# Both layer normalisations scaled on GpSimd, one-input conversions in its splits, and a new table of places

## The chip, the cores and the metric

The kernel runs on one core of a Trainium2 chip. The time is device microseconds of one launch. The time before is a median of 3 runs; the profile is of one further execution.

## The reference, cut to what matters

The input x is 8 batches of 1024 tokens of 256 columns, all in 32 bits. Every batch goes through three layers, each with a residual:

```python
x = x + 0.5 * ffn(layernorm(x), Wq, Wk, Wv, Wo, Wff)      # softmax attention, 16 heads of 16 columns
x = x + attn(layernorm(x), w_qkv, b_qkv, w_o, b_o)        # 8 heads of 32, no softmax
x = x + 0.5 * ffn(layernorm(x), Wq, Wk, Wv, Wo, Wff)

def layernorm(x):  return (x - mean(x)) / sqrt(var(x) + 1e-5)
def ffn(x):        # softmax(q k / 16) v per head, @ Wo, l2 normalise, @ Wff, l2 normalise, exact gelu
def attn(x):       # (q k^T) v per head, @ w_o + b_o
```

The middle layer has no softmax, so the kernel computes it from the Gram matrix of the normalised rows.

## The kernel before

There are 16 phases p. Phases 0 to 7 do the first softmax layer of batches 0 to 7, phases 8 to 15 the last one. A phase has 128 tiles, one for each head and each block of 128 keys, against all 1024 queries. For one tile TensorE makes the scores in a slot of PSUM (`ring`, three slots, line L798 of the profile), VectorE copies them to `exp_ring` and takes their minimum (L636), ScalarE takes the exponential in place and sums it (L563). For each four tiles (a group) VectorE takes the reciprocal of the sums (L646), GpSimd scales the values with it into `v_scaled` (L517, the step `recip` in its order), and TensorE multiplies (`av`, L809) into `o_acc`. `exp_ring` holds four groups, so the scores of a group wait for the product of the group four before.

Beside the tiles of phase p the engines work on its neighbours. For phase p - 1 they do what stands behind the attention: `u` (eight times, TensorE L746 into a slot, ScalarE squares L566 and L569, VectorE copy L653), `u_norm` and `w_norm` (reciprocal roots on GpSimd L524 to L535), `gelu` (ScalarE L574) and `x1` (VectorE L658). For phase p + 1 they do what stands ahead of it: `ln_stats`, `ln_aggr` and `ln_rstd` (VectorE, then one power on GpSimd, L491), `xn` (eight VectorE instructions that normalise `x_prep`, L686), `xt` (transposes L831, ScalarE copy L582), `qk` and `v`. Each `qk` piece of 128x512 is copied to `kq_stage` by ScalarE (L596) and then split on GpSimd into three bf16 parts by four instructions (L397, L399, L401, L403); SyncE's queue copies the parts to `kq_stack` by 32 DMAs for each quarter of a phase (L411). GpSimd does 125 of the 128 splits; ScalarE and VectorE do the other three, at the start.

In phases 1 to 8, called linear here after the name of their table, the middle layer of batch p - 1 is done as well: `ln2_stats`, `ln2_aggr`, `ln2_rstd`, `xn2` (eight VectorE instructions into `w_xn`, L700), `gram` (TensorE, L848, which waits for all eight), `xt2`, `T`, `VK`, `G`, `H`, `xbias` (GpSimd L539) and `y`. Phase 0 and phases 9 to 15 are called plain. The normalisation `xn` is done for phase 0 ahead of the first tile and then in phases 0 to 14.

Nothing is scheduled at run time. Each step has a place in a table (its unit is one tile of the phase), each engine's program is its steps sorted by place less a lead of the engine, and each engine runs its program in order:

```python
            place -= LEAD[engine].get(kind, 0)
            if engine == "pe":
                for part in range(parts):
                    placed.append((place + gap * part, n, part, step))
            else:
                placed.append((place + gap * (parts - 1), n, 0, step))
        return [(step, part) for _, _, part, step in sorted(placed)]
```

Of the kernel before, what the change touches and what calls it, by code (L numbers as in the profile page):

```python
# [5 lines left out]
def build_macaron(nc, x_in, w_qkv, b_qkv, w_o, b_o, Wq, Wk, Wv, Wo, Wff, out):  # L6
# [36 lines left out]
    def tokens(rows):  # L43
# [8 lines left out]
            "ln_stats": (11.5, 15, 15.4, 16.2, 16.3, 16.4, 17.2, 18.9),  # L52
            "ln_aggr": (22.2,),
            "ln_rstd": (28.2,),
            "xn": (31.6, 31.7, 37.7, 39.5, 42.3, 42.4, 55.3, 60.9),
            "xt": (44.7, 49.6),
            "qk": (64.4, 70.9, 72.5, 78.8),
            "v": (86.2, 95.3, 98.3),
            "setup": (66.7,),
            "weights": (103.6, 103.8, 108.6, 111.3),  # L60
            "stack0": (78.4,),
            "load_xp": (8.9,),
        },
        "PLAIN": {
            "recip": 5.7,
            "av": 9,
            "av_next": 2.5,
            "z": 6,
            "u": (8.5, 13, 16.4, 25.1, 32.5, 46.1, 55.5, 60.8),
            "u_norm": (61.9,),  # L70
            "w_norm": (67.5,),
            "gelu": (70.2,),
            "x1": (71.8, 72, 72.1, 72.2),
            "ln_stats": (7.1, 8.4, 9.2, 10, 11.9, 13.3, 13.5, 13.8),
            "ln_aggr": (21,),
            "ln_rstd": (24.2,),
            "xn": (32.3, 34.8, 36.2, 44.9, 45.7, 46.7, 57.1, 60.8),
            "xt": (62.1, 62.3),
            "qk": (78.9, 84.8, 93.3, 102.4, 21, 28.8, 37.5, 41.1),
            "v": (113.9, 119.5, 126.3, 5.4),  # L80
            "load_xp": (1,),
            "stack1": (3.2,),
            "load_xr": (5.4,),
            "stack2": (50.8,),
            "stack3": (60.1,),
            "stack0": (105.3,),
            "store": (109.5,),
# [5 lines left out]
            "z": 6.3,  # L93
            "u": (8.9, 9.9, 15.9, 16.3, 17.4, 22.3, 25.5, 27.6),
            "u_norm": (27.7,),
            "w_norm": (31.3,),
# [18 lines left out]
            "xt": (45.2, 46.3),
            "qk": (77.1, 81.7, 92.8, 97.6, 32.4, 35.9, 38.5, 42.5),
            "v": (111.5, 123.9, 127.1, 7.9),
            "load_xp": (1.9,),
            "stack1": (25.5,),
            "load_xr": (42,),  # L120
            "stack2": (59.3,),
            "stack3": (70.1,),
            "stack0": (100.7,),
            "store": (114.1,),
        },
        "TAIL": {
            "u": (8.4, 10.7, 20, 27.6, 33.6, 51.2, 59.7, 60.2),
            "u_norm": (23.8, 64.1),
            "w_norm": (35.6, 68.8),
            "gelu": (66.9, 90.5),  # L130
            "x1": (79.8, 81.3, 90.5, 96),
            "load_xr": (0.4,),
            "store": (136, 137.5),
        },
# [2 lines left out]
    LEAD = {"sp": {},
            "pe": {},
            "act": {"qk": 1.0, "u": 1.0, "xt2": 1.5, "gram": 1.5, "weights": 3.0, "G": 1.0, "xt": 0.5, "H": 1.5},
            "dve": {"ln_stats": -1.0, "VK": -0.5, "H": 0.5, "z": -0.5},  # L140
            "pool": {"recip": 0.5, "xn": 0.5, "x1": -1.5, "xbias": 2.5, "w_norm": 1.5, "qk": -0.5, "u_norm": -1}}
# [776 lines left out]
```

## Time and profile before

| | |
|---|---|
| median of 3 runs | 2936.62 us (2935.42 to 2938.29) |
| the profiled execution, its own time | 2938.12 us |
| span of its profile | 2936.3 us |
| VectorE busy | 2775.7 us, 95% |
| ScalarE busy | 2704.8 us, 92% |
| TensorE busy (matmuls) | 2692.5 us, 92% |
| GpSimd busy | 857.8 us, 29% |

An engine's busy time is the union of its instructions' records. On VectorE and ScalarE a record reaches some 0.08 us into the next one, so that of instructions without a gap the starts are nearer together than the records are long.

### The profile page before, as it was taken

The page shows a single profiled execution, that of the slowest core. Times are in us where ns is not written, and L with a number is a line of the kernel's source. Part 1 is how long each engine was busy: PE and PEld are TensorE (multiplying, and loading weights), DVE is VectorE, ACT ScalarE, POOL GpSimd, SP SyncE. Part 2 cuts the span into 40 slices and gives each one's busy share as a digit, 9 for nine tenths or more (in the row PEclk, how much of TensorE's full clock was granted, in tenths as well). Part 3 has the DMA queues.
Part 4 walks back from the last instruction along what each step waited for, and adds up shares of the span by engine and source line. Part 5 has one row for each costly group of instructions (what it writes and reads, how often), then busy time and mean ns, then how long its engine had stood idle before and what let it go on. Part 6 is the DMA issues. An engine that isn't in the chain of part 4 may idle for free.

```text
span 2936.3 us, 87317 instructions
## 1 busy us (share of the span) xinstructions
PE 2692.5 (92%) x35680; PEld 1062.6 (36%) x35680; DVE 2775.7 (95%) x5622; ACT 2704.8 (92%) x4983; POOL 857.8 (29%) x1181
## 2 busy tenths in 40 slices
PE   5899999999999999999999998998989899898987
PEld 2233443434434344343343433332333333333422
DVE  5999999999999999999999999999999999999987
ACT  4999998999989989999899999999999999999997
POOL 2323303332133232331323323232331323233121
PEclk8999999999999999999999999999999999999999
DMA  5231242313423234123331243422324342232440
GB/s 122 50 64 41 54 102 48 72 43 59 103 38 58 67 59 101 30 54 81 59 81 39 53 92 59 90 56 57 75 47 102 59 90 56 58 73 47 87 87 16
DMA packets 151362, 192.89 MB, mean 66 GB/s; under 512 B 34001, under 2 KB 85713, under 8 KB 150962
## 3 DMA queue, kind: packets, MB, share of 16 engines
q1 hardware_dynamic: 150386, 186.13, 31.1%
q8 instruction: 281, 4.60, 0.7%
q0 software_dynamic: 576, 1.18, 0.3%
q14 instruction: 119, 0.97, 0.1%
HBM read 36.18 MB, written 16.78 MB: 18 GB/s over the span
## 4 chain that ended last, share of the span: by engine, by line
DVE 41%; PE 26%; ACT 18%; issue 8%; SPq 5%; POOL 1%; DMA 1%; DVEq 0%; POOLq 0%; ACTq 0%
DVE exp_ring L636 33%; ACT exp_ring L563 14%; PE ring L746 10%; PE o_acc L809 7%; PE ring L798 7%; SPq L411 5%; PE ring L848 2%; ACT w_xn L574 2%; DVE bn_stats L676 1%; DVE w_xn L653 1%; DVE x_post L658 1%; DVE v_now L713 1%; DVE w_xn L700 1%; DVE exp_rsums L646 1%; PE ring L831 1%
## 5 line engine op out<-in xcount | busy, mean ns | idle before, releaser
L636 DVE TENSOR_SCALAR_CACHE_REDUCE exp_ring<-ring 128x1024 f32<-128x1024 f32 x2048 | 2411.1, 1213 | 82.9 <-PE ring L798 76.0
L563 ACT ACTIVATE exp_ring<-exp_ring,neg_max 128x1024 f32<-128x1024 f32 x2048 | 2337.4, 1144 | 149.5 <-DVE exp_ring L636 147.5
L798 PE MATMUL ring<-kq_stack 128*32 128x512 bf16 x16384 | 1190.7, 384 | 158.0 <-DVE exp_ring L636 122.6
L809 PE MATMUL o_acc<-exp_ring,v_scaled 128*32 128x512 f32 x8192 | 1079.6, 600 | 27.6 <-POOL v_scaled L517 21.8
L798 PEld LDWEIGHTS ring<-kq_stack 128*32 128x32 bf16 x16384 | 406.1, 96 | 1109.2 <-DVE exp_ring L636 524.8
L517 POOL TENSOR_TENSOR v_scaled<-v_now,exp_rsums 128x64 f32<-128x64 f32 x512 | 151.9, 297 | 1851.8 <-DVE exp_rsums L646 1843.4
L563 ACT ACTIVATION_READ_ACCUMULATOR exp_ring<-exp_ring,neg_max 128x1 f32 x2048 | 386.4, 189 | 0.0
L809 PEld LDWEIGHTS o_acc<-exp_ring,v_scaled 128*32 128x32 f32 x8192 | 251.1, 111 | 249.8 <-POOL v_scaled L517 46.3
L746 PE MATMUL ring<-ffn_wo_wowff,o_T 128*32 128x256 f32 x4096 | 243.9, 380 | 16.6 <-issue 9.1
L746 PE MATMUL ring<-xn_T,ffn_wqkv 128*32 128x512 f32 x2048 | 248.0, 604 | 9.0 <-DVE exp_ring L636 7.7
L746 PEld LDWEIGHTS ring<-ffn_wo_wowff,o_T 128*32 128x32 f32 x4096 | 129.3, 110 | 137.9 <-DVE exp_ring L636 46.0
L636 DVE DVE_READ_ACCUMULATOR exp_ring<-ring 128x1 f32 x2048 | 166.1, 81 | 0.0
L397 POOL TENSOR_TENSOR kq_parts<-kq_stage,zero 128x512 bf16<-128x512 f32 x125 | 129.9, 1039 | 90.3 <-ACT kq_stage L596 76.5
L399 POOL TENSOR_TENSOR kq_rest<-kq_stage,kq_parts 128x512 f32<-128x512 f32 x125 | 148.5, 1188 | 9.8
L403 POOL TENSOR_TENSOR kq_parts<-kq_rest,kq_parts 128x512 bf16<-128x512 f32 x125 | 146.1, 1168 | 9.8
L401 POOL TENSOR_TENSOR kq_parts<-kq_rest,zero 128x512 bf16<-128x512 f32 x125 | 131.1, 1049 | 9.8
L746 PE MATMUL ring<-ffn_wqkv,xn_T 128*32 128x256 f32 x2048 | 122.6, 381 | 7.6 <-DVE exp_ring L636 7.5
L746 PEld LDWEIGHTS ring<-xn_T,ffn_wqkv 128*32 128x32 f32 x2048 | 61.5, 113 | 162.2 <-issue 98.9
L646 DVE RECIPROCAL exp_rsums<-exp_sums 128x4 f32<-128x4 f32 x512 | 87.0, 170 | 2.0 <-ACT exp_ring L563 1.3
L746 PEld LDWEIGHTS ring<-ffn_wqkv,xn_T 128*32 128x32 f32 x2048 | 60.7, 109 | 70.9 <-DVE exp_ring L636 35.0
L596 ACT ACTIVATE kq_stage<-ring 128x512 f32<-128x512 f32 x125 | 72.5, 580 | 8.9 <-PE ring L746 8.9
L653 DVE COPY w_xn<-ring 128x256 f32<-128x256 f32 x128 | 53.2, 415 | 22.4 <-PE ring L746 22.2
(94 smaller groups left out, 1252.6 us busy)
## 6 DMA issues: line engine op xcount, KB each, us to landing
kq_stack<-kq_parts SPq DMA_DIRECT2D x2030, 64.0 KB, 2.4
x_post<-in_L_attn_x SPq DMA_DIRECT2D x8, 1024.0 KB, 6.0
x_slots<-x_post SPq DMA_DIRECT2D x8, 1024.0 KB, 5.4
x_prep<-x_slots SPq DMA_DIRECT2D x8, 1024.0 KB, 9.8
x_post<-x_slots SPq DMA_DIRECT2D x8, 1024.0 KB, 5.9
x_prep<-in_L_attn_x SPq DMA_DIRECT2D x7, 1024.0 KB, 7.8
out<-x_post SPq DMA_DIRECT2D x7, 1024.0 KB, 5.7
kq_stack<-kq_parts POOLq DMA_DIRECT2D x18, 64.0 KB, 4.6
```

Source lines behind the costliest of these rows:

```text
L397: ops.tensor_tensor(hi, piece, zeros, ALU.add).then_inc(done, 1)
L399: ops.tensor_tensor(rest, piece, hi, ALU.subtract).then_inc(done, 1)
L401: ops.tensor_tensor(mid, rest, zeros, ALU.add).then_inc(done, 1)
L403: ops.tensor_tensor(lo, rest, mid, ALU.subtract).then_inc(done, 1)
L411: queue.dma_start(stack[q % 2][FD * t:FD * (t + 1), :, c, :], parts[rows:rows + FD, kp:qp + 4:3 + qp - kp, :]).then_inc(done[q % 2], 16)
L517: nc.gpsimd.tensor_tensor(vsc[a][:, i % EG, :, a * FD:(a + 1) * FD], heads, rsum[:, i % EG, :].unsqueeze(2).to_broadcast([P, HQ, FD]), ALU ...
L563: nc.scalar.activation(e, e, ACT.Exp, bias=negmax[:, i % NM:i % NM + 1], scale=-1.0, accum_out=sums[:, g % EG, c:c + 1]).then_inc(exp_done, 1)
L636: nc.vector.tensor_scalar(E[:, (g % EG) * HQ + c, :].rearrange("p (b n) -> p b n", b=NB), ps, -1.0, None, ALU.mult, ALU.min, accum_out=neg ...
L646: nc.vector.reciprocal(rsum[:, i % EG, :], sums[:, i % EG, :]).then_inc(rsum_ready, 1)
L746: last = mm(out[k:k + COLS], lhsT[:, k:k + COLS], rhs, start=start, stop=stop)
L798: last = mm(ps[k:k + COLS, n, :], kq[:, 0, c, j * P + k:j * P + k + COLS], kq[:, 1, c, n * BANK:(n + 1) * BANK], start=True, stop=True)
L809: last = mm(O[32 * c:32 * c + 32, n, :], vsc[a][:, g % EG, c, :], E[:, (g % EG) * HQ + c, n * BANK:(n + 1) * BANK], start=(a == 0 and j == ...
```

## The change

Five things are changed. `xn` and `xn2` move from VectorE to GpSimd, with the same instruction. The two conversions of a GpSimd split, until now the sum of the piece and a broadcast zero, become one-input instructions (times 1.0, plus 0.0). `XT2` gets a buffer of its own, where it lay in `x_prep`; so the load of `x_prep` no longer waits for the last `y`, and the copy `xt2` waits for the `y` of the phase before it. Half of `kq_rest` goes away; the three first splits use `H` for it. And nearly all places, with some leads, have other numbers.

```diff
         def split(engine, ops, piece, rest, m, n, done, at):
-            zeros = zero[:, 0:1].to_broadcast([P, BANK])
             hi, mid, lo = pieces(m, n)
-            ops.tensor_tensor(hi, piece, zeros, ALU.add).then_inc(done, 1)
+            ops.tensor_scalar(hi, piece, 1.0, 0.0, ALU.mult, ALU.add).then_inc(done, 1)
...
-            ops.tensor_tensor(mid, rest, zeros, ALU.add).then_inc(done, 1)
+            ops.tensor_scalar(mid, rest, 1.0, 0.0, ALU.mult, ALU.add).then_inc(done, 1)
...
-                    if is_linear(p - 3):
-                        sp.wait_ge(filled["y"], nth("pe", "y", p - 3, 3))
...
+                elif kind == "xn":
+                    pool.wait_ge(rstd_ready, p + 1)
+                    nc.gpsimd.tensor_scalar(xp[:, i, :], xp[:, i, :], mv[:, i, 0:1], rstd[:, i:i + 1],
+                                            ALU.subtract, ALU.mult).then_inc(xn_ready, 1)
...
+                elif kind == "xn2":
+                    pool.wait_ge(rstd2_ready, p + 1)
+                    nc.gpsimd.tensor_scalar(wb[:, i, 0:D], xr[:, i, :], mv2[:, i, 0:1], rstd2[:, i:i + 1],
+                                            ALU.subtract, ALU.mult).then_inc(xn2_ready, 1)
...
-                elif kind == "xn":
-                    dve.wait_ge(rstd_ready, p + 1)
-                    nc.vector.tensor_scalar(xp[:, i, :], xp[:, i, :], mv[:, i, 0:1], rstd[:, i:i + 1],
-                                            ALU.subtract, ALU.mult).then_inc(xn_ready, 1)
...
-        XT2 = xp[:].rearrange("p (c t) d -> p c (t d)", c=DC)
+        XT2 = sb("xn2_T", [P, DC, N])
...
                 elif kind == "xt2":
-                    act.wait_ge(filled["xt"], nth("pe", "xt", p + 2, DC - 1))
+                    if p >= 1:
+                        act.wait_ge(filled["y"], nth("pe", "y", p - 1, 3))
...
-            "xn2": (45.5, 46.1, 46.9, 47.1, 47.2, 47.5, 49.4, 49.6),
+            "xn2": (44.1, 44.6, 45.5, 45.7, 45.8, 46.1, 47.8, 48.2),
...
-            "xn": (31.2, 32.7, 33.6, 34, 34, 34, 34.2, 34.4),
+            "xn": (31.1, 31.7, 32.6, 33.9, 33.9, 33.9, 34.1, 36.1),
```

On GpSimd, in the part of the third linear phase in which both norms of the phase before and the first splits are due, the program of before reads as follows (`rstd` is the power of `ln_rstd`, `sumsq_w` and `gelu_scale` are `w_norm`, the four `kq_` rows are one split):

```order
L517 TENSOR_TENSOR v_scaled<-v_now,exp_rsums 128x4x16
L491 TENSOR_TENSOR rstd<-rstd,minus_half 128x8
L533 TENSOR_TENSOR sumsq_w<-sumsq_w,minus_half 128x8
L535 TENSOR_TENSOR gelu_scale<-sumsq_w,u_rnorm 128x8
L397 TENSOR_TENSOR kq_parts<-kq_stage,zero 128x512
L399 TENSOR_TENSOR kq_rest<-kq_stage,kq_parts 128x512
L401 TENSOR_TENSOR kq_parts<-kq_rest,zero 128x512
L403 TENSOR_TENSOR kq_parts<-kq_rest,kq_parts 128x512
L517 TENSOR_TENSOR v_scaled<-v_now,exp_rsums 128x4x16
```

The same part of GpSimd's program after the change reads:

```order
L523 TENSOR_TENSOR v_scaled<-v_now,exp_rsums 128x4x16
L489 TENSOR_TENSOR rstd<-rstd,minus_half 128x8
L492 TENSOR_SCALAR x_prep<-x_prep,bn_mv,rstd 128x256
L539 TENSOR_TENSOR sumsq_w<-sumsq_w,minus_half 128x8
L541 TENSOR_TENSOR gelu_scale<-sumsq_w,u_rnorm 128x8
L492 TENSOR_SCALAR x_prep<-x_prep,bn_mv,rstd 128x256 x2
L397 TENSOR_SCALAR kq_parts<-kq_stage 128x512
L399 TENSOR_TENSOR kq_rest<-kq_stage,kq_parts 128x512
L401 TENSOR_SCALAR kq_parts<-kq_rest 128x512
L403 TENSOR_TENSOR kq_parts<-kq_rest,kq_parts 128x512
L523 TENSOR_TENSOR v_scaled<-v_now,exp_rsums 128x4x16
L492 TENSOR_SCALAR x_prep<-x_prep,bn_mv,rstd 128x256 x5
```

Three of the eight `xn` now stand between two scalings of the values, ahead of the first split, and five behind the second scaling.

Further on in the same phase, from the power of the second normalisation on, GpSimd's program before has one split and then only scalings:

```order
L494 TENSOR_TENSOR rstd<-rstd,minus_half 128x8
L397 TENSOR_TENSOR kq_parts<-kq_stage,zero 128x512
L399 TENSOR_TENSOR kq_rest<-kq_stage,kq_parts 128x512
L401 TENSOR_TENSOR kq_parts<-kq_rest,zero 128x512
L403 TENSOR_TENSOR kq_parts<-kq_rest,kq_parts 128x512
L517 TENSOR_TENSOR v_scaled<-v_now,exp_rsums 128x4x16 x9
```

After the change the eight `xn2` stand among these scalings:

```order
L496 TENSOR_TENSOR rstd<-rstd,minus_half 128x8
L397 TENSOR_SCALAR kq_parts<-kq_stage 128x512
L399 TENSOR_TENSOR kq_rest<-kq_stage,kq_parts 128x512
L401 TENSOR_SCALAR kq_parts<-kq_rest 128x512
L403 TENSOR_TENSOR kq_parts<-kq_rest,kq_parts 128x512
L523 TENSOR_TENSOR v_scaled<-v_now,exp_rsums 128x4x16
L499 TENSOR_SCALAR w_xn<-x_post,bn_mv,rstd 128x256 x7
L523 TENSOR_TENSOR v_scaled<-v_now,exp_rsums 128x4x16
L499 TENSOR_SCALAR w_xn<-x_post,bn_mv,rstd 128x256
L523 TENSOR_TENSOR v_scaled<-v_now,exp_rsums 128x4x16 x7
```

Seven of them run in one piece, with one scaling behind them and the eighth behind that.

VectorE's program at that place, between two reciprocals, read so before:

```order
L646 RECIPROCAL exp_rsums<-exp_sums 128x4
L700 TENSOR_SCALAR w_xn<-x_post,bn_mv,rstd 128x256
L636 TENSOR_SCALAR exp_ring,neg_max<-ring 128x1024
L700 TENSOR_SCALAR w_xn<-x_post,bn_mv,rstd 128x256 x2
L636 TENSOR_SCALAR exp_ring,neg_max<-ring 128x1024
L700 TENSOR_SCALAR w_xn<-x_post,bn_mv,rstd 128x256 x3
L636 TENSOR_SCALAR exp_ring,neg_max<-ring 128x1024 x2
L700 TENSOR_SCALAR w_xn<-x_post,bn_mv,rstd 128x256
L646 RECIPROCAL exp_rsums<-exp_sums 128x4
```

After the change only the tiles are left between such reciprocals, over more than five groups of four; two of the groups are:

```order
L653 RECIPROCAL exp_rsums<-exp_sums 128x4
L643 TENSOR_SCALAR exp_ring,neg_max<-ring 128x1024 x4
L653 RECIPROCAL exp_rsums<-exp_sums 128x4
L643 TENSOR_SCALAR exp_ring,neg_max<-ring 128x1024 x4
L653 RECIPROCAL exp_rsums<-exp_sums 128x4
```

In SyncE's queue the plain phases now issue `load_xr` ahead of the quarter `stack1`, and the store of the output ahead of `stack0` of the next phase; the linear phases keep their order there.

## Rows read from the trace of the kernel before

**Rows 1.** The page: busy time, share of the span and instructions.

```profile
PE 2692.5 (92%) x35680; PEld 1062.6 (36%) x35680; DVE 2775.7 (95%) x5622; ACT 2704.8 (92%) x4983; POOL 857.8 (29%) x1181
```

**Rows 2.** Windows: halves of a linear and a plain phase; columns as headed.

```profile
core 0: us, PE busy (x) PEld busy (x) DVE busy (x) ACT busy (x) POOL busy (x), PEclk, DMA share, GB/s
782.87:885.80 102.93, 95.63 (x1211) 39.58 (x1207) 98.09 (x214) 92.36 (x180) 30.03 (x39) 0.97 0.28 55
885.80:970.49 84.69, 83.49 (x1190) 35.07 (x1186) 81.97 (x156) 79.28 (x137) 27.21 (x36) 1.00 0.35 75
2064.58:2151.41 86.83, 81.44 (x1112) 31.31 (x1104) 84.86 (x181) 83.39 (x165) 27.74 (x38) 1.00 0.32 63
2151.41:2236.02 84.61, 75.21 (x960) 25.64 (x960) 81.12 (x156) 82.49 (x144) 22.30 (x32) 0.96 0.36 75
```

**Rows 3.** Waits, 782.87 to 885.80: us in total, times, longest.

```profile
ACT exp_ring L563 <- DVE exp_ring L636: 6.4, 10, 1.8
PE ring L798 <- DVE exp_ring L636: 3.4, 6, 1.1
DVE exp_ring L636 <- PE ring L798: 2.3, 4, 1.2
PE o_acc L809 <- POOL v_scaled L517: 2.2, 2, 1.9
```

**Rows 4.** Groups by line, same stretch: busy us, mean ns, idle before.

```profile
L686 DVE TENSOR_SCALAR x_prep<-x_prep,bn_mv,rstd 128x256 f32<-128x256 f32 x8 | 4.7, 631 | 0.0
L700 DVE TENSOR_SCALAR w_xn<-x_post,bn_mv,rstd 128x256 f32<-128x256 f32 x8 | 3.6, 475 | 0.0
L658 DVE SCALAR_TENSOR_TENSOR x_post<-w_xn,x_post 128x512 f32<-128x512 f32 x4 | 3.1, 781 | 0.0
```

**Rows 5.** Timeline of VectorE, then GpSimd, 824 to 830: start, us, what.

```profile
826.50 3.38 DVE L686 TENSOR_SCALAR x_prep<-x_prep,bn_mv,rstd 128x256 f32<-128x256 f32 x5
829.80 0.68 DVE L658 SCALAR_TENSOR_TENSOR x_post<-w_xn,x_post 128x512 f32<-128x512 f32 x1
...
825.36 1.17 POOL L399 TENSOR_TENSOR kq_rest<-kq_stage,kq_parts 128x512 f32<-128x512 f32 x1
826.61 1.19 POOL L401 TENSOR_TENSOR kq_parts<-kq_rest,zero 128x512 bf16<-128x512 f32 x1
827.88 1.15 POOL L403 TENSOR_TENSOR kq_parts<-kq_rest,kq_parts 128x512 bf16<-128x512 f32 x1
829.11 0.29 POOL L517 TENSOR_TENSOR v_scaled<-v_now,exp_rsums 128x64 f32<-128x64 f32 x1
```

**Rows 6.** Groups by line of a plain half, 2064.58 to 2151.41.

```profile
L686 DVE TENSOR_SCALAR x_prep<-x_prep,bn_mv,rstd 128x256 f32<-128x256 f32 x8 | 3.3, 412 | 0.0
```

**Rows 7.** Groups by line, whole span, GpSimd alone.

```profile
L517 POOL TENSOR_TENSOR v_scaled<-v_now,exp_rsums 128x64 f32<-128x64 f32 x512 | 151.9, 297 | 1851.8 <-DVE exp_rsums L646 1843.4
L397 POOL TENSOR_TENSOR kq_parts<-kq_stage,zero 128x512 bf16<-128x512 f32 x125 | 129.9, 1039 | 90.3 <-ACT kq_stage L596 76.5 <-DMA kq_stack<-kq_parts 13.4
L539 POOL TENSOR_TENSOR x_post<-x_post,bias_wide 128x512 f32<-128x512 f32 x32 | 40.9, 1288 | 16.7 <-DVE bias_wide L733 16.7
L491 POOL TENSOR_TENSOR rstd<-rstd,minus_half 128x8 f32<-128x8 f32 x16 | 26.3, 1643 | 6.9 <-DVE rstd L683 6.4
L485 POOL MEMSET v_scaled<- 128x512 f32 x2 | 1.0, 520 | 0.0
L480 POOL MEMSET identity<- 128x128 f32 x1 | 0.2, 201 | 0.0
```

**Rows 8.** Timeline of the start, VectorE and TensorE.

```profile
10.56 2.67 DVE L686 TENSOR_SCALAR x_prep<-x_prep,bn_mv,rstd 128x256 f32<-128x256 f32 x8 [1.85 <-POOL rstd L491]
11.12 4.07 PE L831 MATMUL ring<-identity,x_prep 128*128 128x128 f32 x16 [11.12 <-DVE x_prep L686]
```

**Rows 9.** Timeline of GpSimd, 819 to 857, first and last of interest.

```profile
819.88 1.64 POOL L491 TENSOR_TENSOR rstd<-rstd,minus_half 128x8 f32<-128x8 f32 x1
...
856.44 0.37 POOL L517 TENSOR_TENSOR v_scaled<-v_now,exp_rsums 128x64 f32<-128x64 f32 x1 [5.06 <-DVE exp_rsums L646]
```

More of the change, by code:

```diff
@@ L51, in build_macaron @@
         "START": {
[L52 to L62, printed above, removed]
+            "ln_stats": (12.7, 16.2, 16.6, 17.5, 17.6, 18.1, 18.4, 20.1),
@@ L63, in build_macaron @@
+            "ln_aggr": (26.8,),
+            "ln_rstd": (33.2,),
+            "xn": (35.1, 35.2, 40.4, 43, 45.8, 46.1, 58.8, 64.4),
+            "xt": (39.6, 45.6),
+            "qk": (64.5, 72.5, 74.5, 82.8),
+            "v": (88.2, 93.7, 97.6),
+            "setup": (60.2,),
+            "weights": (106.3, 107.2, 108.7, 113.8),
+            "stack0": (83.8,),
+            "load_xp": (11.3,),
         },
         "PLAIN": {
-            "recip": 5.7,
+            "recip": 5.4,
             "av": 9,
@@ L67, in build_macaron @@
             "av_next": 2.5,
-            "z": 6,
+            "z": 5.8,
             "u": (8.5, 13, 16.4, 25.1, 32.5, 46.1, 55.5, 60.8),
[L70 to L87, printed above, removed]
+            "u_norm": (61.8,),
+            "w_norm": (69.7,),
+            "gelu": (70.4,),
+            "x1": (71.8, 71.8, 72, 72.1),
+            "ln_stats": (6.5, 7.8, 8.9, 9.7, 11.6, 16.5, 16.7, 19.3),
@@ new lines, in build_macaron @@
+            "ln_aggr": (21.4,),
+            "ln_rstd": (26,),
+            "xn": (33.8, 34, 35.4, 44.1, 44.9, 48.5, 56.3, 60),
+            "xt": (61.1, 62.1),
+            "qk": (78.9, 84.8, 93.3, 102.4, 21.2, 28.9, 37.7, 41.3),
+            "v": (114.1, 119.7, 126.5, 5.9),
+            "load_xp": (0.1,),
+            "stack1": (4.3,),
+            "load_xr": (3.5,),
+            "stack2": (50.5,),
+            "stack3": (71.6,),
+            "stack0": (124,),
+            "store": (119.7,),
@@ L92, in build_macaron @@
             "av_next": 2,
[L93 to L96, printed above, removed]
+            "z": 5.1,
+            "u": (8.9, 9.9, 15.3, 16.3, 17.4, 22.3, 25.5, 27.6),
+            "u_norm": (27.9,),
+            "w_norm": (31.7,),
             "gelu": (32.6,),
-            "x1": (34.7, 35.4, 35.8, 36.6),
-            "ln2_stats": (36.4, 36.6, 37.3, 37.9, 38.1, 38.3, 38.4, 39),
+            "x1": (34.7, 35.5, 36, 36.6),
@@ L112, in build_macaron @@
-            "ln_aggr": (27.5,),
-            "ln_rstd": (29.6,),
-            "xn": (31.2, 32.7, 33.6, 34, 34, 34, 34.2, 34.4),
[L115 to L124, printed above, removed]
+            "ln2_rstd": (41.2,),
@@ new lines, in build_macaron @@
+            "xn2": (44.1, 44.6, 45.5, 45.7, 45.8, 46.1, 47.8, 48.2),
+            "gram": (52.4, 58.3),
+            "xt2": (65.9, 101.1),
+            "T": (63.1,),
+            "VK": (70.3,),
+            "G": (72.4,),
+            "H": (87.7,),
+            "xbias": (89.2, 90.3, 113.2, 115.7),
+            "y": (103.2, 107, 115.5, 119),
+            "ln_stats": (9.3, 14.5, 15.7, 16.1, 17.7, 20.7, 23.2, 26.4),
+            "ln_aggr": (27.4,),
+            "ln_rstd": (29.8,),
+            "xn": (31.1, 31.7, 32.6, 33.9, 33.9, 33.9, 34.1, 36.1),
@@ L125, in build_macaron @@
+            "xt": (44.3, 45.4),
+            "qk": (77.5, 81.7, 92.8, 97.6, 31.9, 35.9, 38.5, 41.1),
+            "v": (111.4, 123.8, 127, 7.9),
+            "load_xp": (10.8,),
+            "stack1": (25.4,),
+            "load_xr": (48.5,),
+            "stack2": (56.3,),
+            "stack3": (66.8,),
+            "stack0": (96.1,),
+            "store": (109,),
         },
         "TAIL": {
-            "u": (8.4, 10.7, 20, 27.6, 33.6, 51.2, 59.7, 60.2),
-            "u_norm": (23.8, 64.1),
@@ L129, in build_macaron @@
[L129 to L133, printed above, removed]
+            "u": (7.6, 8, 17.9, 25.7, 34.8, 52.6, 62, 62.2),
+            "u_norm": (19.1, 64.2),
+            "w_norm": (36.7, 68.8),
+            "gelu": (69.4, 89.1),
+            "x1": (72, 73, 82.2, 86.1),
+            "load_xr": (1.6,),
+            "store": (133.6, 137.6),
         },
     }
-    GAP = {'gram': 0.5, 'G': 0.5}
+    GAP = {'gram': 0.5, 'G': 1.0}
@@ L137, in build_macaron @@
     LEAD = {"sp": {},
             "pe": {},
[L139 to L141 removed]
+            "act": {"qk": 1.0, "u": 1.0, "xt2": 1.5, "gram": 2.5, "weights": 3.5, "G": 1.0, "xt": 1.0, "H": 1.0},
+            "dve": {"VK": -0.5, "z": -1.0, "w_norm": 1},
@@ L142, in build_macaron @@
+            "pool": {"recip": 0.5, "xn": 0.5, "x1": -1.5, "xbias": 2.0, "w_norm": 1.0, "qk": -0.5, "u_norm": -0.5, "xn2": -1}}
     AHEAD = {"xt": DC, "qk": 4, "v": 3}
@@ L503, in _ @@
                             pool.wait_ge(stacked[k], stack_count(q[0], q[1] + k))
-                    split(pool, nc.gpsimd, qstage[:, staged((kind, p, i)) % 2, :], resid[:, 0, :], m, n,
+                    split(pool, nc.gpsimd, qstage[:, staged((kind, p, i)) % 2, :], resid[:], m, n,
                           split_step, SPLIT_STEPS * (POOL_SPLITS[kind, p, i] - 1))
```

24 lines of the change are left out of this document (6 added, 18 removed).

## The prediction

> **What bounds the kernel now.** I read the page first: VectorE is busy 95% of the span, ScalarE and TensorE 92% each, GpSimd 29% [rows 1]. Three engines are near full and one is nearly free, so the question is not whether VectorE is loaded but what stands right behind it when it is relieved. The average hides that, so I cut one linear and one plain phase into their halves at VectorE's copies of `o_acc`, which stand once each 64 tiles [rows 2]. The reader is to see four stretches with four different limits. The first half of a linear phase takes 102.93 us; VectorE is busy 98.09 of it, TensorE 95.63, ScalarE 92.36. The second half takes 84.69 with TensorE at 83.49, so TensorE sets it alone. The first half of a plain phase takes 86.83, with VectorE at 84.86 and ScalarE at 83.39. The second half takes 84.61, with ScalarE at 82.49. Both normalisations lie in the first halves. The waits of the first linear half say the same [rows 3]: TensorE waited 3.4 us for VectorE to empty a slot, ScalarE 6.4 us for VectorE, and VectorE only 2.3 us for TensorE. TensorE also waited 2.2 us for `v_scaled` of GpSimd.
>
> **What VectorE loses.** A record of VectorE overlaps the next by about 0.08 us: eight `xn` at the start span 2.67 us, 0.33 each [rows 8], where a record has 0.412 [rows 6]. In a linear phase `xn` has 0.631 and `xn2` 0.475 [rows 4], so the phase loses 8 x (0.631 - 0.08) + 8 x (0.475 - 0.08) = 4.4 + 3.2 = 7.6 us of VectorE. A plain phase loses 8 x (0.412 - 0.08) = 2.7 us. There are 8 linear phases and 7 plain ones with an `xn` (phase 15 prepares nothing): 61 + 19 = 80 us, and 2.7 at the start.
>
> Why `xn` costs more in a linear phase can be seen in one place [rows 5]. Five of them took 3.38 us instead of 1.7, and they ended only after GpSimd's L401 and L403 had ended, one after the other. On GpSimd the wait of one engine for the other goes away with the VectorE instruction. The Trainium skill has a rule for it (SBUF — State Buffer, Who interferes with whom): a VectorE instruction in a two-port mode, or one with two SBUF inputs against a GpSimd instruction that reads SBUF, and a GpSimd instruction shut each other out for the whole of an instruction. The trace agrees for `xn`, with the 3.38 us. By that rule `x1`, which reads `w_xn` and `x_post`, could now wait for the new `xn` behind which it stands. The row of `x1` in a linear phase has 0.781 where an undisturbed one has 0.68 [rows 4, 5]; four of them with one GpSimd instruction of 0.45 us in the way of each would cost at most 1.8 us a phase. The sum would be 8 x 1.8 = 14 us less gain with all of it on the path. I count none of it, since VectorE has room after the change.
>
> **What GpSimd gets.** The trace has no one-input arithmetic on GpSimd, so I bound it [rows 7]. A memset has no input: 0.201 us for 128 columns and 0.520 for 512, so 0.83 ns a column and 0.095 fixed. A two-input instruction has 0.297 for 64 columns and 1.288 for 512: 2.2 ns a column and 0.155 fixed. An `xn` of 256 columns is thus between 0.31 and 0.72 us, a conversion of 512 between 0.52 and 1.04 (it will hardly be slower than the two-input form that it replaces). I take 0.45 and 0.70, nearer to the memset, as a read and a write of one stream each can overlap. A rule of the skill is against the change as a whole (GPSIMD Engine Reference, Engine selection): elementwise work belongs on VectorE, GpSimd being about twice slower for two inputs and about at line rate for one. The rows give at worst 0.72 against VectorE's 0.33. What decides is whether GpSimd's slower instruction is on a path.
>
> In a linear phase GpSimd's crowded stretch runs from 819.88, the power of `ln_rstd`, to 856.44, the scaling ahead of which seven `xn2` stand [rows 9]: 36.6 us. Its work there after the change is two powers and `w_norm` (3 x 1.64 + 0.2 = 5.1), four splits of 2 x 0.70 + 1.19 + 1.17 and 0.3 of gaps, 4.1 each (16.2 against 18.2 before, from 2 x 1.04), six scalings (1.8), eight `xn` (3.6) and seven `xn2` (3.2): 29.9 us. It fits. With the upper prices it is 5.1 + 18.2 + 1.8 + 15 x 0.72 = 35.9, just within. `gram` waits for the last `xn2`; on VectorE that one stood right behind the reciprocal of the scaling at 856.44 [rows 9], so it ended at about that time, and on GpSimd it comes with 29.9 us of work from 819.88, at the same place or sooner. So `xn`, `xn2` and the splits cost nothing in the likeliest case, hidden behind 36 us of tiles. Without that cover each 1 us of lateness would be 8 us.
>
> The 2.2 us that TensorE waits for `v_scaled` stay. The scaling that ran at 829.11 had its reciprocal from VectorE before the five `xn` of 826.50, and stood behind a split [rows 5]. After the change three `xn` (1.35) stand ahead of it as well and the split is 0.7 shorter: 0.6 later at worst, or none where GpSimd had waited for `w_norm` anyway. I count zero.
>
> **What is gained.** VectorE's first linear half falls from 98.09 to 90.5. TensorE is then the fullest with 95.63, and its gaps are 102.93 - 95.63 = 7.3 us. Of these 3.4 are waits for VectorE at the scores [rows 3], and some 0.6 more are such waits at other matmuls (an estimate, as they are smaller groups). I take these 4.0 as the gain of a linear phase: 8 x 4.0 = 32 us. It can't be more than 7.3, nor more than VectorE's 7.6. The second halves, set by TensorE or ScalarE and without a normalisation, gain nothing. In a plain phase VectorE's first half falls to 82.2, and ScalarE is the fullest with 83.39. The stretch is now 2.0 us longer than its fullest engine is busy; with the same 2.0 it takes 85.4 and gains 1.4: 7 x 1.4 = 10 us.
>
> **What is lost.** At the start TensorE's transposes follow `xn` one by one [rows 8]. On GpSimd eight take 8 x 0.45 = 3.6 instead of 2.67, so the first tile is 0.9 us later (between 0 and 3.1). The other edits cost nothing: the loads and stores moved in SyncE's queue are single DMAs whose data is needed tens of microseconds later; the load of `x_prep` still stands behind the store that waits for the last `y`, so losing its wait changes no time, which the order of the queue shows; and the last steps behind the last tile stand in the same order on every engine.
>
> The sum is 32 + 10 - 0.9 = 41 us. The profiled execution took 2938.1, its span 2936.3 and 1.8 around it; it lies 1.5 over the median. So 2938.1 - 41 = 2897, and on the median 2896 us, 1.4% less.
>
> **The rivals.**
>
> *Everything follows VectorE.* The waits of TensorE and ScalarE could be ripples of VectorE's stalls, longer than what is recorded as waiting, since a matmul record also covers its drain. Then each phase shortens by all that VectorE loses: 2936.6 - 80 + 1 = 2858. For it: ScalarE's 6.4 us of waiting. Against it: TensorE's 95.63 in a linear half, which allows 7.3 only with no gap left.
>
> *Balance eats it.* With VectorE at 90.5, ScalarE at 92.4 and TensorE at 95.6 coupled through three slots, new waits take most of what is freed, as in the second plain half, where no engine is over 82.5 and the stretch takes 84.61. An `x1` held up by GpSimd is one such wait. The gain would be some 1.5 us a linear phase and 0.5 a plain one: 2936.6 - 15 = 2921.
>
> *GpSimd becomes late (slower than before).* If `xn` costs more than I bound it at, the seven `xn2` in one piece hold the scaling behind them and `gram` behind the last. The stretch of 36.6 us is full at 5.1 + 16.2 + 1.8 + 15c = 36.6, c = 0.90 us. Each 0.1 over it costs 1.5 us in each of 8 phases; against a gain of 5.1 per linear phase (41/8) it decides from c = 0.90 + 5.1/15 = 1.24 us. At 1.5 us it would be 8 x 9 = 72 slower less 41 gained: 2968. Against it: no elementwise row of GpSimd of this width is over 0.72.
>
> *The change does nothing measurable*, because of the 2.2 us waits for `v_scaled` growing by what the rest gains (4 us more a phase at one spot, four groups of `exp_ring` deep): about 2936.
>
> **The numbers.** Forecast 0.60, everything follows 0.13, balance 0.16, late GpSimd 0.07, nothing 0.04. The likeliest case's own range is 2880 to 2912. The range that holds 8 in 10 takes in part of both neighbours: 2862 to 2924. What can be told from no change here is 0.2%, 6 us. Faster 0.89, same 0.04, slower 0.07.
>
> **What the profile after would show.** VectorE's busy time is some 80 us less, near 2690, and L643 alone stands between reciprocals; the linear first half takes about 99 us with TensorE the fullest; GpSimd's `xn` rows are 0.31 to 0.72 us and its conversions 0.52 to 1.04; the 3.4 us of L798's waits for VectorE fall below half; the second halves keep 84.7 and 84.6. I am wrong in size if the second halves move by over 1 us, or if the waits of `o_acc` for `v_scaled` grow beyond some 30 us, and wrong in kind if an `xn` on GpSimd takes over 0.9 us.

## The result and the profile after

The changed kernel takes 2996.12 us (median of 4 runs, 2993.51 to 2997.58) against 2937.45 us beside it: ratio 1.0199, 95% interval 1.0181 to 1.0217. It is 2% slower, where the prediction said 1.4% faster. The page of its profile has a span of 2991.1 us and this line of busy times (columns as in [rows 1]):

```profile
PE 2705.5 (90%) x35680; PEld 1084.0 (36%) x35680; DVE 2706.2 (90%) x5430; ACT 2691.5 (90%) x4983; POOL 994.7 (33%) x1373
```

VectorE lost 70 us of work (I had put it at 80; `x1` alone takes 5.5 us more than before, 50.8 for 45.3), and the kernel still got slower. The windows of the same two halves, which answer to [rows 2], show where:

```profile
814.08:924.07 109.99, 96.81 (x1211) 41.34 (x1207) 91.88 (x198) 91.28 (x180) 46.92 (x55) 0.95 0.26 51
924.07:1008.93 84.86, 83.66 (x1190) 35.07 (x1194) 81.98 (x158) 79.62 (x137) 23.99 (x36) 1.00 0.36 76
1008.93:1121.26 112.33, 99.01 (x1211) 41.96 (x1207) 91.87 (x200) 91.27 (x180) 46.95 (x55) 0.92 0.25 49
2131.26:2216.77 85.51, 80.39 (x1104) 32.08 (x1104) 81.97 (x173) 83.13 (x166) 34.12 (x46) 1.00 0.30 55
2216.77:2300.55 83.78, 75.12 (x960) 25.97 (x960) 81.35 (x156) 81.66 (x145) 19.02 (x32) 0.96 0.40 88
```

The plain halves are 1.3 and 0.8 us shorter, the second linear half is unchanged, and these two first linear halves are 7.1 and 9.4 us longer (over all eight they take 109.2 to 112.4 us). In them no engine is near full any more: TensorE, the fullest, is busy 88%. The waits of the first of these stretches name the cause; the line of 2.2 us of [rows 3] has become 12.1:

```profile
DVE exp_ring L643 <- PE ring L797: 14.3, 8, 5.9
PEld o_acc L808 <- POOL v_scaled L523: 13.6, 3, 6.0
PE o_acc L808 <- POOL v_scaled L523: 12.1, 3, 5.5
ACT gram_then_vk L608 <- PE ring L847: 7.2, 1, 7.2
```

VectorE's 14.3 us and ScalarE's 7.2 us are waits for TensorE; in the kernel with cheap norms below they come to 3.3 and 1.9 in such a half, so they follow from TensorE's own waits. The groups by line, GpSimd alone, whole span, give the price that the prediction had to guess, beside [rows 7]:

```profile
L492 POOL TENSOR_SCALAR x_prep<-x_prep,bn_mv,rstd 128x256 f32<-128x256 f32 x128 | 160.0, 1256 | 1.8
L499 POOL TENSOR_SCALAR w_xn<-x_post,bn_mv,rstd 128x256 f32<-128x256 f32 x64 | 77.6, 1226 | 0.0
L397 POOL TENSOR_SCALAR kq_parts<-kq_stage 128x512 bf16<-128x512 f32 x125 | 77.6, 620 | 62.7 <-ACT kq_stage L603 51.2 <-DMA kq_stack<-kq_parts 11.2
L401 POOL TENSOR_SCALAR kq_parts<-kq_rest 128x512 bf16<-128x512 f32 x125 | 81.5, 652 | 11.1
```

The conversions are where I put them (0.62 and 0.65; I took 0.70). The norms are at 1.25, far over the bounds of 0.31 to 0.72. The timelines of GpSimd and TensorE in the first of these stretches show what that does; they answer to [rows 5] and [rows 9]:

```profile
855.65 2.43 POOL L492 TENSOR_SCALAR x_prep<-x_prep,bn_mv,rstd 128x256 f32<-128x256 f32 x2
...
862.75 0.62 POOL L523 TENSOR_TENSOR v_scaled<-v_now,exp_rsums 128x64 f32<-128x64 f32 x1
863.36 6.55 POOL L492 TENSOR_SCALAR x_prep<-x_prep,bn_mv,rstd 128x256 f32<-128x256 f32 x5
...
873.78 0.29 POOL L523 TENSOR_TENSOR v_scaled<-v_now,exp_rsums 128x64 f32<-128x64 f32 x1
...
885.04 8.47 POOL L499 TENSOR_SCALAR w_xn<-x_post,bn_mv,rstd 128x256 f32<-128x256 f32 x7
893.48 0.30 POOL L523 TENSOR_TENSOR v_scaled<-v_now,exp_rsums 128x64 f32<-128x64 f32 x1
```

```profile
863.42 1.93 PE L808 MATMUL o_acc<-exp_ring,v_scaled 128*32 128x512 f32 x8 [5.51 <-POOL v_scaled L523]
...
874.13 1.94 PE L808 MATMUL o_acc<-exp_ring,v_scaled 128*32 128x512 f32 x8 [3.13 <-POOL v_scaled L523]
...
878.92 1.03 PE L808 MATMUL o_acc<-exp_ring,v_scaled 128*32 128x512 f32 x8
...
893.83 1.91 PE L808 MATMUL o_acc<-exp_ring,v_scaled 128*32 128x512 f32 x8 [3.49 <-POOL v_scaled L523]
```

Three scalings of the values stand behind a run of norms: three of them and a split, five of them and a split, and the seven `xn2`. TensorE waited for each. The reader is to see the 1.93, 1.94 and 1.91 too: the same eight matmuls take 1.03 where no such wait stands before them. The granted clock over the three slow groups is 0.50, 0.50 and 0.52, over the quick one that starts at 866.73 it is 1.00: behind each of these waits TensorE ran at 1.2 GHz, not 2.4. The granted clock of the two first linear halves is 0.95 and 0.92, against 0.97 in [rows 2].

### The profile page after: what moved, and what is told of

Read it like the earlier page. It is cut to its first block, busy times and chain, and to the rows that moved or that the text cites. A ratio compares the mean times of both kernels' runs of the same rounds, so it can differ in the third digit from the quotient of the medians.

```text
span 2991.1 us, 87310 instructions
## 1 busy us (share of the span) xinstructions
PE 2705.5 (90%) x35680; PEld 1084.0 (36%) x35680; DVE 2706.2 (90%) x5430; ACT 2691.5 (90%) x4983; POOL 994.7 (33%) x1373
## 4 chain that ended last, share of the span: by engine, by line
DVE 34%; PE 29%; ACT 16%; POOL 10%; issue 7%; SPq 3%; DMA 1%; DVEq 0%; POOLq 0%; ACTq 0%
DVE exp_ring L643 29%; ACT exp_ring L569 14%; PE ring L745 11%; PE o_acc L808 8%; PE ring L797 8%; SPq L411 3%; POOL x_prep L492 3%; POOL w_xn L499 2%; PE ring L847 2%; DVE bn_stats L683 1%; POOL kq_rest L399 1%; PE ring L830 1%; POOL kq_parts L403 1%; ACT w_xn L580 1%; DVE v_now L712 1%
## 5 line engine op out<-in xcount | busy, mean ns | idle before, releaser
L808 PE MATMUL o_acc<-exp_ring,v_scaled 128*32 128x512 f32 x8192 | 1091.5, 606 | 104.6 <-POOL v_scaled L523 99.0
L797 PEld LDWEIGHTS ring<-kq_stack 128*32 128x32 bf16 x16384 | 418.2, 97 | 1063.3 <-DVE exp_ring L643 449.5
L492 POOL TENSOR_SCALAR x_prep<-x_prep,bn_mv,rstd 128x256 f32<-128x256 f32 x128 | 160.0, 1256 | 1.8
L397 POOL TENSOR_SCALAR kq_parts<-kq_stage 128x512 bf16<-128x512 f32 x125 | 77.6, 620 | 62.7 <-ACT kq_stage L603 51.2
L401 POOL TENSOR_SCALAR kq_parts<-kq_rest 128x512 bf16<-128x512 f32 x125 | 81.5, 652 | 11.1
```

Source lines behind the costliest of these rows:

```text
L401: ops.tensor_scalar(mid, rest, 1.0, 0.0, ALU.mult, ALU.add).then_inc(done, 1)
L492: nc.gpsimd.tensor_scalar(xp[:, i, :], xp[:, i, :], mv[:, i, 0:1], rstd[:, i:i + 1], ALU.subtract, ALU.mult).then_inc(xn_ready, 1)
L797: last = mm(ps[k:k + COLS, n, :], kq[:, 0, c, j * P + k:j * P + k + COLS], kq[:, 1, c, n * BANK:(n + 1) * BANK], start=True, stop=True)
L808: last = mm(O[32 * c:32 * c + 32, n, :], vsc[a][:, g % EG, c, :], E[:, (g % EG) * HQ + c, n * BANK:(n + 1) * BANK], start=(a == 0 and j == ...
```

## The experiments

My theory after this profile: the price of a norm on GpSimd alone makes the loss, by holding up the scalings. The rivals: the new places are at fault; the price is not GpSimd's own but contention; or GpSimd in this chain is late at any price.

**GpSimd alone.** The same instruction in several forms, each four times and each awaited, nothing beside it.

> Not the kernel, but GpSimd alone, one instruction at a time, with nothing on VectorE; the output is a plain copy of the input. Forms of arithmetic on 128 x 64, 256 and 512 columns of f32: two operands that are columns in SBUF (the form of xn), two constants, one column, one constant, a broadcast column as second tensor, two tensors, and two constants with a bf16 result. Theory of the price: the form with two columns costs 1.2 us at 256 and grows with the width, while two constants cost about half of the 512-wide conversion of 0.62, 0.35 us. Rival of contention: alone, the form with two columns costs 0.31 to 0.72 us as I had bounded it, and the 1.26 us of the profile come from the work beside it.

Measured, groups by line with the shapes kept apart:

```profile
L40 POOL TENSOR_SCALAR two_columns<-src,src_two 128x256 f32<-128x256 f32 x4 | 4.9, 1218 | 0.4
L42 POOL TENSOR_SCALAR two_constants<-src 128x256 f32<-128x256 f32 x4 | 4.3, 1069 | 0.3
L50 POOL TENSOR_TENSOR two_tensors<-src,src_two 128x256 f32<-128x256 f32 x4 | 2.9, 722 | 0.3
L52 POOL TENSOR_SCALAR two_constants_bf<-src 128x256 bf16<-128x256 f32 x4 | 1.6, 404 | 0.3
```

Contention is out: alone the form has 1.218. But my expectation of 0.35 for two constants missed too: 1.069. A column in place of a constant costs only 0.15. The two constants with a bf16 result (0.404) differ in two things at once, the type and the pair of operations.

**Both norms on VectorE again, xn2 alone, xn alone**, each on the changed kernel. The edit of the first, shown for `xn` and the same for `xn2`; each of the other two makes one half of it:

```diff
-                elif kind == "xn":
-                    pool.wait_ge(rstd_ready, p + 1)
-                    nc.gpsimd.tensor_scalar(xp[:, i, :], xp[:, i, :], mv[:, i, 0:1], rstd[:, i:i + 1],
-                                            ALU.subtract, ALU.mult).then_inc(xn_ready, 1)
...
+                elif kind == "xn":
+                    dve.wait_ge(rstd_ready, p + 1)
+                    nc.vector.tensor_scalar(xp[:, i, :], xp[:, i, :], mv[:, i, 0:1], rstd[:, i:i + 1],
+                                            ALU.subtract, ALU.mult).then_inc(xn_ready, 1)
```

> The changed kernel with xn and xn2 on VectorE again; its places, its conversions and its own buffer stay. Theory of the price: the losses all hang on the two norms on GpSimd, so this is no slower than before, 2925 to 2938 us. Rival of the places: the new table is what costs the time, and this stays at 2970 to 2996.

> The changed kernel with xn2 alone on VectorE again. Theory of the price with three waits a linear phase (5.5, 3.1 and 3.5 us): the last of the three goes with its slow matmuls behind it, some 4.5 us, and VectorE gets 3.2 back: 2996 - 8 x 4 = 2964. If the waits are worth only what VectorE is charged, 2996.

> The changed kernel with xn alone on VectorE again, xn2 on GpSimd. Theory of the price: the start gets 7.4 us back, each linear phase its first two waits of 8.6 and some 2 of slow clock less 3 for VectorE's share, each plain phase loses about 1.5: 2996 - 7 - 60 + 10 = 2939. Rival of the places: over 2970.

Measured: 2927.97 us with both back (ratio to before 0.9968, 0.9957 to 0.9980), 2966.15 with `xn2` back (1.0093, 1.0076 to 1.0110), 2965.58 with `xn` back (1.0098, 1.0083 to 1.0113). With both back the changed kernel is a little faster than the one before: the places and the conversions are not at fault, and the whole loss of 68 us hangs on the two moves. They share it about evenly. The first linear halves take 101.7 us with both on VectorE, 107.0 to 108.1 with `xn` on GpSimd, 106.1 to 106.8 with `xn2` there, and 109 to 112 with both. With `xn` back I had expected 2939, and 27 us more were measured. I had taken 7.6 us off each first linear half, 8.6 of waits and 2 of slow clock less 3 for VectorE, and some 4.5 came off. The waits for `v_scaled` went nearly as expected, from 12.1 us in a linear half to 4.1 (34.5 over the whole span, in 9 waits, the longest 4.2). But TensorE now waited 2.4 us for VectorE at the scores and 2.3 for ScalarE's `kq_stage` in their place, against 0.8 and none. So the waits that were taken away gave back only about half of their length.

**Which operations.** More forms alone on GpSimd.

> GpSimd alone again, other forms, 64 and 256 columns; the output is a plain copy of the input. In the first such run subtract-then-multiply with two constants took 1.07 us at 256 columns with an f32 result, and multiply-then-add with 1.0 and 0.0 only 0.40 with a bf16 result. Either the pair of operations makes the difference, then multiply-then-add is at 0.40 with f32 results and with columns too (some 0.55), and the norm could be written so; or the bf16 result makes it, then all pairs with f32 results are near 1.1 us and all with bf16 near 0.40; or the values 1.0 and 0.0 are special.

Measured, the same view, 256 columns, seven of the rows (the view cuts off the front of long names; `btract_` is `subtract_`):

```profile
L51 POOL TENSOR_SCALAR subtract_mult_columns<-src,src_two 128x256 f32<-128x256 f32 x4 | 4.9, 1221 | 0.4
L51 POOL TENSOR_SCALAR mult_subtract_columns<-src,src_two 128x256 f32<-128x256 f32 x4 | 4.9, 1222 | 0.4
L51 POOL TENSOR_SCALAR btract_mult_constants_bf<-src 128x256 bf16<-128x256 f32 x4 | 4.3, 1070 | 0.3
L51 POOL TENSOR_SCALAR mult_add_columns<-src,src_two 128x256 f32<-128x256 f32 x4 | 2.2, 556 | 0.4
L51 POOL TENSOR_SCALAR mult_add_constants<-src 128x256 f32<-128x256 f32 x4 | 1.6, 406 | 0.3
L51 POOL TENSOR_SCALAR add_mult_constants<-src 128x256 f32<-128x256 f32 x4 | 1.6, 406 | 0.3
L53 POOL TENSOR_TENSOR subtract_broadcast<-src,src_two 128x256 f32<-128x256 f32 x4 | 2.5, 612 | 0.3
```

It is the pair of operations. With constants a pair with a subtraction costs 1.07, and multiplication with addition, in either order, 0.41, each the same with an f32 as with a bf16 result. Columns in place of constants add 0.15 to either: 1.22 and 0.56. A subtraction of two tensors is not slow (0.612). The multiply-then-add form with columns lies inside the bounds of the prediction.

**The conversions alone**, on the kernel before.

```diff
-            ops.tensor_tensor(hi, piece, zeros, ALU.add).then_inc(done, 1)
+            ops.tensor_scalar(hi, piece, 1.0, 0.0, ALU.mult, ALU.add).then_inc(done, 1)
```

> The kernel before with the one-input conversions alone. Theory of the price: each of 125 splits is 0.8 us shorter, and of TensorE's 2.2 us of waiting for v_scaled in a linear phase about half goes: 2937 - 8 = 2929. If the split is hidden everywhere: 2937.

Measured: 2943.63 us, 1.0018 (1.0009 to 1.0027). I had expected 2929, or 2937 if the split is hidden everywhere. Less work on GpSimd made the kernel slightly slower, which neither side expected. TensorE's waits for `v_scaled` did fall, from 21.8 us over the span to 7.5, and nothing came of it. The linear first halves keep their 102.3 to 103.4 us, but the plain ones go from 87 to 88.1. There, in VectorE's timeline and GpSimd's, a first `xn` of a plain phase now takes 0.92 us where it took 0.48 before:

```profile
2105.39 0.92 DVE L685 TENSOR_SCALAR x_prep<-x_prep,bn_mv,rstd 128x256 f32<-128x256 f32 x1
...
2104.98 1.17 POOL L402 TENSOR_TENSOR kq_parts<-kq_rest,kq_parts 128x512 bf16<-128x512 f32 x1
```

It ended at 2106.31, 0.16 after GpSimd's L402. Another `xn` of the phase takes 0.82 against 0.41, likewise until GpSimd's L402 has ended. Both lie on VectorE, the fullest engine there: some 0.8 us more a phase, in 7 phases 6 us. The split moved under them by finishing sooner. So this is the exclusion of [rows 5], by chance of the meeting. The profile shows 2.2 us more at the start, and these are not the conversions': the first 64 matmuls of `qk` took 9.19 us instead of 7.07, and the first 16 of them, started from 16.61 on, were twice as slow (3.4 us for 1.7), before GpSimd began its first split at 21.00. Over the traces of this case the 64 take between 7.07 and 9.72, so a difference of some 2 us at the start of one trace can't be put down to a change of the kernel. The split's speed is worth nothing where the split is hidden.

**The moves with the old places.** The kernel before, only with both norms on GpSimd.

> The kernel before with both norms on GpSimd, the two-input conversions and the old places. Theory of the price: the splits are 0.8 us longer than in the changed kernel and the queue of GpSimd is later still, 2996 + 8 x 2 = 3012. Rival of the places: with the old places it is near 2940.

Measured: 3039.86 us, 1.0343 (1.0329 to 1.0357), first linear halves of 114.3 to 116.1. The new places and shorter conversions together take 44 us off this loss; they are the opposite of its cause. I had given them 16.

**xn on GpSimd in the plain phases only**, the rest on VectorE, on the changed kernel.

```diff
-                elif kind == "xn":
+                elif kind == "xn" and p > 0 and table(p - 1) is TABLES["PLAIN"]:
...
+                elif kind == "xn" and not (p > 0 and table(p - 1) is TABLES["PLAIN"]):
+                    dve.wait_ge(rstd_ready, p + 1)
```

> The changed kernel with xn on GpSimd in the plain phases only; in the linear phases and at the start xn, and xn2 everywhere, are on VectorE. Theory of the price: GpSimd has room in a plain phase even at 1.25 us, and a plain first half is 1.2 us shorter than with xn on VectorE (85.6 against 86.8): 2928 - 7 x 1.2 = 2920. If the plain phases lose elsewhere what they gain there: 2928.

Measured: 2915.41 us, 0.9925 (0.9912 to 0.9937); the plain first halves take 85.0 to 86.0 instead of 86.8 in nearly all phases. Even at 1.22 us an `xn` on GpSimd pays where its queue has room. The gain of 12.6 is more than the 8 expected. The first plain halves account for 9.4 of it. The profile can't place the rest: the profiled execution took 2921.40 us, 6 us over the median, and is only 7 us below that of the kernel with both norms on VectorE.

**The norm as multiply-then-add.** The changed kernel, with x * rstd + (-mean * rstd):

```diff
...
+                    nc.gpsimd.tensor_tensor(shift[:, 0, :], mv[:, :, 0], rstd[:], ALU.mult).then_inc(shifted, 1)
+                    pool.wait_ge(shifted, 2 * p + 1)
+                    nc.gpsimd.tensor_scalar(shift[:, 1, :], shift[:, 0, :], -1.0, 0.0,
+                                            ALU.mult, ALU.add).then_inc(shifted, 1)
...
-                    nc.gpsimd.tensor_scalar(xp[:, i, :], xp[:, i, :], mv[:, i, 0:1], rstd[:, i:i + 1],
-                                            ALU.subtract, ALU.mult).then_inc(xn_ready, 1)
+                    nc.gpsimd.tensor_scalar(xp[:, i, :], xp[:, i, :], rstd[:, i:i + 1], shift[:, 1, i:i + 1],
+                                            ALU.mult, ALU.add).then_inc(xn_ready, 1)
```

> The changed kernel with the norm written as x times rstd plus (minus mean times rstd), so that both norms on GpSimd are multiply-then-add with two columns; 0.45 us of small instructions per norm make the new column. Alone that form took 0.556 us at 256 columns where subtract-then-multiply took 1.22. Theory of the price: the waits of the linear phases go, the first linear halves come to 98 to 99 us, the plain ones stay at 85.5: against the kernel with both norms on VectorE (2928) 8 x 3 and 7 x 1.3 less, and 3 more at the start: 2898. If what matters is that GpSimd stands in the chain at all, and not its price, it stays over 2960.

Measured: 2900.01 us, 0.9869 (0.9854 to 0.9884), 96 us less than the changed kernel, with the same places, from the price of 192 instructions alone. Its windows of a linear phase, its two price rows, and the one wait left, with the run of seven `xn2`:

```profile
776.60:875.92 99.32, 93.81 (x1215) 40.18 (x1211) 92.08 (x198) 91.77 (x180) 36.79 (x59) 0.98 0.28 56
875.92:960.58 84.66, 83.46 (x1190) 34.94 (x1186) 81.97 (x156) 78.97 (x137) 23.94 (x36) 1.00 0.37 76
```

```profile
L503 POOL TENSOR_SCALAR x_prep<-x_prep,rstd,shift 128x256 f32<-128x256 f32 x128 | 77.5, 615 | 1.7
L517 POOL TENSOR_SCALAR w_xn<-x_post,rstd,shift 128x256 f32<-128x256 f32 x64 | 34.8, 563 | 0.0
```

```profile
842.41 3.79 POOL L517 TENSOR_SCALAR w_xn<-x_post,rstd,shift 128x256 f32<-128x256 f32 x7
...
824.02 1.93 PE L826 MATMUL o_acc<-exp_ring,v_scaled 128*32 128x512 f32 x8 [3.60 <-POOL v_scaled L541]
```

Of the three waits the one behind the first three `xn` and the split is left, 3.60 us for 5.51. So GpSimd in the chain is not late at any price, and the theory of the price holds: expected were 2898 us, and over 2960 if the price did not matter.

**The same with the old START table and the first eight xn on VectorE**, and **the moves in the multiply-add form on the kernel before, with its places and conversions**, and **the changed kernel with both norms on VectorE and the old START table**:

> The same with the eight xn of the start on VectorE and the START table of before. By the records of the start: 2.7 against 4.5 us for the eight xn, and 2 to 4 us from the old order of the first steps: 2893, if the last theory holds for the rest.

> The kernel before with both norms on GpSimd in the multiply-add form, its two-input conversions and its old places. Theory of the price: the sum of GpSimd's crowded stretch is 5.1 + 0.9 + 18.2 + 1.8 + 15 x 0.56 = 34.4 of 36.6 us, just full; some lateness is left, 2915. If the new places carry the gain: at or over 2937.

> The changed kernel with both norms on VectorE and the START table of before. Its first tile came 4.4 us later than before; if that is the order of the new START table, 2928 - 4 = 2924; if it is TensorE's clock at the start, which is the same for both, 2928.

Measured in that order: 2894.45 us, 0.9854 (0.9841 to 0.9868), the fastest of all; 2934.23 us, 0.9986 (0.9978 to 0.9995); 2925.59 us, 0.9960 (0.9947 to 0.9972). For the second I had expected 2915, and it came within 3 us of the rival, that the new places carry the gain (at or over 2937). With the old places and conversions the cheap norms are worth almost nothing: the first linear halves take 101.8 to 102.9, hardly less than before, TensorE's 3.4 us of waiting for VectorE having become 3.8 to 6.8 us of waiting for `v_scaled`. With the new ones they are worth 28 us. But the new places don't carry the gain alone either: with both norms on VectorE they and the conversions gave 10 us. It takes both. How much of it is the places and how much the shorter split, which takes 3.3 us out of GpSimd's crowded stretch, no run separates. The start is worth 2 to 6 us, from the order of its steps and from where its `xn` run.

## Why the prediction was wrong, point by point

**The step that failed** is the bound of a norm on GpSimd: "An `xn` of 256 columns is thus between 0.31 and 0.72 us". It took the two-input instruction for the upper end, by the thought that fewer inputs can't cost more. On it rest the 29.9 us of GpSimd's stretch, and with them the step "`xn`, `xn2` and the splits cost nothing in the likeliest case". The runs put 1.22 alone and 1.25 in the kernel in its place, by the operations of the instruction and not its inputs. The trace of before had no row of a one-input instruction with a subtraction, and I named GpSimd's late queue as a rival but gave it 7 in 100, because "no elementwise row of GpSimd of this width is over 0.72". That was misread: [rows 7] has no row of this width at all, and the 0.72 was my own line drawn between 64 and 512 columns.

**The rival's own sum was too mild as well.** It put the point of decision at 1.24 us, so that with 1.25 the kernel should have been as fast as before; it was 59 us slower. That sum asked whether the work of the whole stretch fits in 36.6 us. With the measured prices the work is 5.1 + 15.6 + 1.8 + 15 x 1.25 = 41 us, some 5 too much, and TensorE's waits came to 12.1 in a linear phase, in the stretch shown each followed by matmuls at the lower clock. The scalings inside the stretch have due times of their own, four tiles apart, and each of the three waits stands behind a run of norms that passes them. So beside the load of the queue the longest run counts that stands ahead of an instruction for which another engine waits. That is read from where the waits stand; no run spread the same norms at the same price. (A slip in the prediction's sum changes nothing here: four splits of before are 19.0 us with the gaps that it counts, not 18.2, so that its upper total is 36.7, just over the 36.6 and not just within.)

**The gain was sized well once the price is right.** The multiply-add kernel has the price that I assumed (0.56 and 0.61 for my 0.45), and takes 2900 where I forecast 2896. Its parts: a plain first half with an `xn` gains 1.4 us against both norms on VectorE (86.8 to some 85.4 in the mean; forecast 1.4); a linear one 2.3 from the moves (101.7 to 99.4 in the mean of eight) and 1.2 from places and conversions (102.9 to 101.7), 3.5 together against my 4.0. That the total lies within 4 us is luck in part: places and conversions gave 1.2 of the 3.5 and I had counted nothing for them, the first copy of `o_acc` comes 3.7 us later for my 0.9, and the second plain halves give back 3 us for which I had no term. That TensorE would be the next limit is right: it is busy 93.81 of 99.32, VectorE 92.08. That VectorE's relief is not worth its whole length, but half or less, is right too: 28 us for 65.5 (2770.4 to 2704.9).

**The wait of 2.2 us for `v_scaled` "stays".** It did not: 12.1 in the changed kernel, and still 3.6 with the cheap norms, as three norms stand ahead of it. Over the whole span these waits grew from 21.8 to 99.0 us, past the 30 that the prediction names as a sign of being wrong in size. With both norms back on VectorE they are nearly gone (1.8 us over the span). The shorter split alone, on the old places, took them from 21.8 to 7.5, and the new places the rest. I had counted zero for either.

**The start** cost 8 us, not 0.9: the first copy of `o_acc` comes at 149.21 instead of 141.01. Eight norms took 10.05 us for 2.67; with both norms on VectorE the same point is at 144.04, and with the old START table as well at 141.30. So some 5 us are the norms and some 3 the START table, each known to a microsecond or two only, by the 64 matmuls of above (8.46 us in the changed kernel, 7.07 before).

**The rule on GpSimd and VectorE** (the Trainium skill, SBUF — State Buffer, Who interferes with whom) was to hold up `x1`. It agrees with what the runs show, though not behind the norms: in the changed kernel's first linear half two of the four `x1` take 1.11 and 1.20 us instead of 0.68 (before, one of four took 1.1), and beside both stand instructions of the split and the scaling behind it. VectorE had room. I had not thought of the other side: GpSimd was held up too, on the very run that TensorE awaited. The first three rows are GpSimd's there, which take 1.16, 0.62 and 0.29 with nothing beside them:

```profile
858.75 1.47 POOL L399 TENSOR_TENSOR kq_rest<-kq_stage,kq_parts 128x512 f32<-128x512 f32 x1
860.32 1.12 POOL L401 TENSOR_SCALAR kq_parts<-kq_rest 128x512 bf16<-128x512 f32 x1
862.75 0.62 POOL L523 TENSOR_TENSOR v_scaled<-v_now,exp_rsums 128x64 f32<-128x64 f32 x1
...
858.09 1.11 DVE L665 SCALAR_TENSOR_TENSOR x_post<-w_xn,x_post 128x512 f32<-128x512 f32 x1 [1.56 <-ACT w_xn L580]
862.02 1.20 DVE L665 SCALAR_TENSOR_TENSOR x_post<-w_xn,x_post 128x512 f32<-128x512 f32 x1
```

Together that is 1.1 us of the wait of 5.51. The same rule fits the two longer `xn` of the kernel with the conversions alone. The other rule (the Trainium skill, GPSIMD Engine Reference, Engine selection), about twice slower for two inputs and line rate for one, would have been the right warning, but its reason is not what is seen here: the form with one input was the slow one, 1.22 us for 256 columns against 0.72 with two tensors.

**What stays open.** Why a TENSOR_SCALAR with a subtraction is slow on GpSimd was not tried further. The other pairs of operations were not measured. Each form was timed in one execution. The share of the places and that of the shorter split in the gain are not separated, and neither are the load of GpSimd's queue and the length of its runs.

## What to carry to other kernels

Before work is moved to an engine, measure that very instruction there, with its operations and operands: rows of instructions that look alike bounded this one wrong by a factor of 1.7, and rewriting x - m times r as x times r plus a prepared column halved it. When a queue with room takes on more work, add up not only its load but also the longest run that stands ahead of each instruction for which a full engine waits, and place such runs between two of them. A freed engine gives back only the distance to the next one, here about 28 us for 65 freed, and only with places and splits made for it: with the old ones the same moves gave 4.

## What the runs showed of the hardware that I had not expected

On GpSimd a TENSOR_SCALAR of 256 columns costs 0.406 us as multiply-add or add-multiply with constants, 0.556 with columns, but 1.07 and 1.22 in the two pairs with a subtraction that were tried; for 512 columns subtract-then-multiply takes 1.92 with constants and 2.07 with columns. One operation alone is slow too, a product with one constant 0.847 and with one column 0.922 for 256 columns, slower than the pair of multiplication and addition, and slower than a product with a broadcast column as second tensor (0.612). From 256 to 512 columns the multiply-add costs 0.83 ns a column more (0.404 to 0.617 us), as much as the memset of [rows 7], two tensors 2.1, the single product 2.5 and the pair with a subtraction 3.3.

TensorE's clock: after the waits of 5.51, 3.13, 3.49 and 3.60 us of the stretches shown the next eight matmuls took 1.91 to 1.94 us; after one of 1.92 us in the kernel before they took 1.06. The length of the wait does not decide it alone. In the multiply-add kernel the same wait of 3.60 us stands in eight linear phases: behind it the eight matmuls took 1.93 us in four of them, 1.77, 1.53 and 1.26 in three, and 1.06 in one, at a granted clock of 0.50 to 1.00. Such a wait cost up to 0.9 us more here, and sometimes nothing.
